# Even and odd projection columns in two tiles, values in long rows, the normalised input stored once: one change to a transformer layer on one core

## The reference

```
xn = (x - mean) / sqrt(var + 1e-5)
q, k, v = split(xn @ Wq + bq), split(xn @ Wk + bk), split(xn @ Wv + bv)
rope(x) = x * cos + rot(x) * sin          # rot: (even, odd) -> (-odd, even)
weights = softmax(rope(q) @ rope(k).T / sqrt(256))
attention = (weights @ v) @ Wo + bo
h = relu(s0 * [xn, -xn] @ w0) * 2;  h = relu(s1 * h @ w1) * 2;  ffn = s2 * h @ w2
out = x + attention + ffn
```

## Time and profile before

| | us |
|---|---|
| three runs | 2738.41, 2738.48, 2739.38 (median 2738.48) |
| the profiled run | 2738.91 |
| its span, first to last instruction | 2737.1 |

### The profile page before, as it was taken

One profiled execution on the slowest core, in us unless ns is written; L12 is line 12 of the kernel. 1 busy time (PEld: TensorE's weight loads), 2 busy tenths in 40 slices (PEclk: granted clock), 3 DMA queues, 4 the chain that ended last, 5 costly groups with the idle time before them and its releaser, 6 DMA issues.

```text
span 2737.1 us, 49717 instructions
## 1 busy us (share of the span) xinstructions
PE 2648.9 (97%) x21063; PEld 1397.6 (51%) x21063; DVE 989.5 (36%) x1655; ACT 2083.9 (76%) x2301; POOL 299.0 (11%) x265
## 2 busy tenths in 40 slices
PE   7999499999999999999999999999999999999997
PEld 5777245454444445454545454454545454544544
DVE  7776232324242323232342334242423323242322
ACT  4556388888888887878787878888787878787883
POOL 4666100000000000000000000000000000000000
PEclk9999699999999999999999999999999999999998
DMA  8888412212222222222221222221222222222213
GB/s 256 256 259 252 114 38 55 53 52 59 59 59 59 73 54 72 55 60 72 57 71 55 72 67 75 57 77 51 73 63 55 68 60 67 63 75 59 81 26 112
DMA packets 288416, 228.67 MB, mean 84 GB/s; under 512 B 184128, under 2 KB 227904, under 8 KB 281664
## 3 DMA queue, kind: packets, MB, share of 16 engines
q1 hardware_dynamic: 279744, 217.08, 29.0%
q10 hardware_dynamic: 8448, 8.39, 0.9%
HBM read 140.46 MB, written 84.93 MB: 82 GB/s over the span
## 4 chain that ended last, share of the span: by engine, by line
PE 86%; issue 1%; SPq 1%; DMA 1%; DVE 0%; POOLq 0%; POOL 0%; DVEq 0%
PE ps_o L930 35%; PE ps_f L963 26%; PE ps_s L915 23%; PE ps_y L978 2%; PE ps_f L1020 0%; SPq L810 0%; DMA xT_lo<-xn_lo_d 0%; DMA probs<-rest_sum_d 0%; PE ps_y L1020 0%; DVE k_rows L1115 0%; PE ps_o L1020 0%; SPq L807 0%; DVE sums L1060 0%; DMA heads_t<-heads 0%; SPq L709 0%
## 5 line engine op out<-in xcount | busy, mean ns | idle before, releaser
L895 ACT ACTIVATE probs<-ps_s 128x1024 f32<-128x1024 f32 x2048 | 1930.0, 1033 | 472.4 <-PE ps_s L915 470.1
L930 PE MATMUL ps_o<-probs,v_ones 128*32 128x512 f32 x8192 | 1011.9, 600 | 0.0
L915 PE MATMUL ps_s<-q_rows,k_rows 50*128 50x512 f32 x4096 | 866.3, 439 | 31.8 <-DMA q_rows<-row_shift 31.0
L915 PEld LDWEIGHTS ps_s<-q_rows,k_rows 50*128 50x128 f32 x4096 | 365.0, 184 | 701.9 <-ACT probs L895 600.0
L1077 DVE COPY raw<-ps_f 128x512 f32<-128x512 f32 x256 | 165.0, 686 | 790.8 <-PE ps_f L963 790.8
L930 PEld LDWEIGHTS ps_o<-probs,v_ones 128*32 128x32 f32 x8192 | 200.7, 109 | 418.5 <-issue 296.0
L963 PE MATMUL ps_f<-h_hi,ffn_w 64*128 64x512 f32 x2048 | 406.9, 393 | 0.0
L963 PE MATMUL ps_f<-h_lo,ffn_w 64*128 64x512 f32 x2048 | 405.8, 391 | 0.0
L1039 POOL TENSOR_TENSOR heads<-heads,sums 128x512 f32<-128x512 f32 x64 | 82.4, 1288 | 2147.9 <-DVE sums L1060 2147.9
L1060 DVE RECIPROCAL sums<-sums 128x128 f32<-128x128 f32 x256 | 226.7, 924 | 1.7
L963 PEld LDWEIGHTS ps_f<-h_lo,ffn_w 64*128 64x128 f32 x2048 | 195.8, 186 | 37.3
(11 more groups left out here) (102 smaller groups left out, 1616.5 us busy)
## 6 DMA issues: line engine op xcount, KB each, us to landing
k_rows<-k_parts SPq DMA_DIRECT2D x128, 256.0 KB
q_rows<-q_parts SPq DMA_DIRECT2D x384, 64.0 KB
q_parts<-parts SPq DMA_DIRECT2D x32, 512.0 KB, 3.7
k_parts<-parts SPq DMA_DIRECT2D x32, 512.0 KB, 5.5
k_rows<-k_parts SPq DMA_DIRECT2D x128, 128.0 KB
x_chunk<-in_x ACTq DMA_DIRECT2D x16, 512.0 KB, 6.0
xn_hi_d<-xn_hi SPq DMA_DIRECT2D x16, 512.0 KB, 4.4
xn_lo_d<-xn_lo SPq DMA_DIRECT2D x16, 512.0 KB, 5.2
```

The lines of the kernel that those rows point to most:

```text
L895: nc.scalar.activation(probs[:, s % PBUF, half * 2 * C:(half + 1) * 2 * C], ps_s[:, half].rearrange("p c n -> p (c n)"), ACT.Exp, scale=SC ...
L915: last = nc.tensor.matmul(ps_s[:, half, w], k_rows[rows, u, t * P:(t + 1) * P], q_rows[rows, u, half], start=True, stop=True)
L930: last = nc.tensor.matmul(ps_o[32 * c:32 * c + 2 * DH], v_ones[:, u, t], probs[:, s % PBUF, c * C:(c + 1) * C], start=(t == 0), stop=(t == ...
```

## The change

**Columns.** The weights are stored by even and odd columns: tile m = 0 holds the even, m = 1 the odd columns of all heads. One projection gives both tiles, in the two banks of ps_p, and each is the other's partner: `turned` is even x cos - odd x sin, then odd x cos + even x sin. The crossed copy of the weights and its projection go. A head is now 8 rows of the even and 8 rows of the odd tile, at two places of each scratch tensor, and `load_rows` reads them so. The order of a q tile's column blocks is permuted (COLUMNS) so that a half of the queries is one row of 4 KB.

**x.** ACT makes one more copy of the transposed x in float32 (`copy_x`), which is stored and loaded once. In attention DVE makes hi and lo of it (`split_x`) in round 24 of the pass before, and once ahead of the passes.

**v.** It has a PSUM bank of its own and is computed in two halves; its rows are stored 4 KB long, and each head's v is loaded by four DMAs.

**Statistics and FFN weights.** bn_aggr replaces five small DVE operations; statistics run one chunk further ahead; the FFN's weights are made in chunks 4 to 11, an eighth in each.

```diff
+FFN_WEIGHTS_AT = 4
+COLUMNS = [CB // 2 * (r % 2) + r // 2 for r in range(CB)]
+SPLIT_AT = 2 * len(BURSTS) + 4
...
             def store_x(c):
                 u = c % 2
-                sp.wait_ge(x_split, c + 1)
-                sp.dma_start(hi_out[c], x_hi[:, u].bitcast(F32)).then_inc(x_stored[u], 16)
-                sp.dma_start(lo_out[c], x_lo[:, u].bitcast(F32)).then_inc(x_stored[u], 16)
+                sp.wait_ge(x_copied, c + 1)
+                sp.dma_start(scratch["xn"][c], x_t[:, u].rearrange("p k n -> p (k n)")).then_inc(x_stored[u], 16)
...
+            def copy_x(c):
+                u = c % 2
+                if c >= 2:
+                    act.wait_ge(x_stored[u], 16 * (c // 2))
+                nc.scalar.activation(x_t[:, u].rearrange("p k n -> p (k n)"), ps_t[:].rearrange("p k n -> p (k n)"),
+                                     ACT.Copy).then_inc(x_copied, 1)
...
                 if n >= 2:
-                    pe.wait_ge(products_ready, n - 1)
-                for swapped in range(2):
+                    pe.wait_ge(products_ready, 2 * n - 2)
+                for m in range(2):
                     for k in range(DT):
-                        at = slice((j % DT) * P, (j % DT + 1) * P)
-                        w_hi, w_lo = wqk_hi[:, swapped, j // DT, k, at], wqk_lo[:, swapped, j // DT, k, at]
-                        to = ps_p[:, n % 2, swapped]
+                        w_hi, w_lo = wqk_hi[:, of, k, m], wqk_lo[:, of, k, m]
+                        to = ps_p[:, n % 2, m]
...
             for c in range(NC):
-                project(4 * c)
-                values(c)
+                project(2 * c)
+                if c + 1 < NC:
+                    turn(c + 1)
+                values(c, 0)
+                project(2 * c + 1)
+                values(c, 1)
                 if c > 0:
                     lengths(c - 1)
-                project(4 * c + 1)
-                project(4 * c + 2)
-                if c + 1 < NC:
-                    turn(c + 1)
-                project(4 * c + 3)
...
+                for t in range(TT):
+                    last = nc.vector.bn_aggr(moments[:, u, t], stats[:, u, t])
+                last.then_inc(var_ready, 1)
...
 def heads_of(scratch):
-    return (scratch[name].rearrange("a (g d) n -> g a d n", d=DH) for name in ("k", "q"))
+    return (scratch[name].rearrange("am (g e) n -> g am e n", e=HALF) for name in ("k", "q"))
...
         sp.dma_start(k_rows[at:at + 2 * DH, :].bitcast(F32), k_head[g]).then_inc(loaded, 16)
-        sp.dma_start(k_rows[at + 2 * DH:at + AUG, :].bitcast(F32), k_head[g, 0]).then_inc(loaded, 16)
-        sp.dma_start(q_rows[at:at + DH].bitcast(F32), q_half[g, 0, w]).then_inc(loaded, 16)
-        sp.dma_start(q_rows[at + DH:at + 2 * DH].bitcast(F32), q_half[g, 0, w]).then_inc(loaded, 16)
-        sp.dma_start(q_rows[at + 2 * DH:at + AUG].bitcast(F32), q_half[g, 1, w]).then_inc(loaded, 16)
-        sp.dma_start(q_rows[at + AUG:at + ROWS].bitcast(F32), shift[g, w]).then_inc(loaded, 16)
+        sp.dma_start(k_rows[at + 2 * DH:at + AUG, :].bitcast(F32), k_head[g, 0:2]).then_inc(loaded, 16)
+        sp.dma_start(q_flat[at:at + DH].bitcast(F32), q_head[g, 0:2, :, here]).then_inc(loaded, 16)
+        sp.dma_start(q_flat[at + DH:at + 2 * DH].bitcast(F32), q_head[g, 0:2, :, here]).then_inc(loaded, 16)
+        sp.dma_start(q_flat[at + 2 * DH:at + AUG].bitcast(F32), q_head[g, 2:4, :, here]).then_inc(loaded, 16)
+        sp.dma_start(q_flat[at + AUG:at + ROWS].bitcast(F32), shift[g, w]).then_inc(loaded, 16)
...
             def load_v(g, u):
-                sp.dma_start(v_ones[:, u, :, 0:DH], v_src[g]).then_inc(v_loaded[u], 16)
+                for r in range(CB):
+                    sp.dma_start(v_ones[:, u, r * TT:(r + 1) * TT, 0:DH], v_src[CB * (g // H) + r, :, g % H]).then_inc(v_loaded[u], 16)
 
             def load_x(i):
-                sp.dma_start(xT_hi[:].bitcast(F32), hi_src[i]).then_inc(xT_loaded, 16)
-                sp.dma_start(xT_lo[:].bitcast(F32), lo_src[i]).then_inc(xT_loaded, 16)
+                sp.dma_start(xT_lo[:].bitcast(F32).rearrange("p k n -> p (k n)"), scratch["xn"][i]).then_inc(xT_loaded, 16)
...
+            def split_x(i):
+
+                dve.wait_ge(xT_loaded, 16 * (i + 1))
+                nc.vector.tensor_copy(xT_hi[:], xT_lo[:].bitcast(F32)).then_inc(xT_high, 1)
+                dve.wait_ge(xT_high, i + 1)
+                nc.vector.tensor_tensor(xT_lo[:], xT_lo[:].bitcast(F32), xT_hi[:].bitcast(F32), ALU.subtract).then_inc(xT_split, 1)
...
+                    if n == SPLIT_AT and not last:
+                        split_x(i + 1)
```

More of the change, by code:

```diff
@@ L366, in _ @@
             high(0)
+            copy_x(0)
             deviation(1)
+            normalise(1)
+            deviation(2)
             act.wait_ge(weights_loaded, 16 * 6)
@@ L441, in lengths @@
                 for j in range(4):
-                    last = nc.tensor.matmul(ps_n[32 * j:32 * j + 32], per_head[:], square[:, c % 2, j], start=True, stop=True)
+                    rows = slice(32 * (j // 2), 32 * (j // 2 + 1))
+                    last = nc.tensor.matmul(ps_n[rows], per_head[:], square[:, c % 2, j], start=(j % 2 == 0), stop=(j % 2 == 1))
                 last.then_inc(norm_done, 1)
@@ L466, in _ @@
             pool.wait_ge(w_high, 1)
-            nc.gpsimd.tensor_tensor(wqk_lo[:, 0], wqk[:], wqk_hi[:, 0].bitcast(F32), ALU.subtract)
-            plain, crossed = (x.rearrange("p n k (m two) -> p n k m two", two=2) for x in (wqk[:], wqk_hi[:, 1]))
-            crossed_lo = wqk_lo[:, 1].rearrange("p n k (m two) -> p n k m two", two=2)
-            for side in range(2):
-                nc.gpsimd.tensor_tensor(crossed_lo[..., side], plain[..., 1 - side], crossed[..., side].bitcast(F32), ALU.subtract)
+            for m in range(2):
+                for n in range(2):
+                    nc.gpsimd.tensor_tensor(wqk_lo[:, n, :, m], of_pairs[:, n, :, :, m], wqk_hi[:, n, :, m].bitcast(F32), ALU.subtract)
             nc.gpsimd.tensor_tensor(wv_lo[:], wv[:], wv_hi[:].bitcast(F32), ALU.subtract).then_inc(w_split, 1)
@@ L483, in _ @@
                     pool.wait_ge(parts_ready, n - 2)
-                nc.gpsimd.tensor_tensor(turned[:, n % 3], by_cos[:, u], by_sin[:, u], ALU.add).then_inc(turn_done, 1)
+                nc.gpsimd.tensor_tensor(turned[:, n % 3], by_cos[:, u], by_sin[:, u], ALU.add if n % 2 else ALU.subtract).then_inc(turn_done, 1)
                 if n > 0:
@@ L574, in _ @@
             dve.wait_ge(weights_loaded, 16 * 6)
-            nc.vector.tensor_copy(wqk_hi[:, 0], wqk[:])
-            plain = wqk[:].rearrange("p n k (m two) -> p n k m two", two=2)
-            crossed = wqk_hi[:, 1].rearrange("p n k (m two) -> p n k m two", two=2)
-            for side in range(2):
-                nc.vector.tensor_copy(crossed[..., side], plain[..., 1 - side])
+            for m in range(2):
+                for n in range(2):
+                    nc.vector.tensor_copy(wqk_hi[:, n, :, m], of_pairs[:, n, :, :, m])
             nc.vector.tensor_copy(wv_hi[:], wv[:]).then_inc(w_high, 1)
-            nc.vector.stream_shuffle(bqk[:, 1], bqk[:, 0], [i ^ 1 for i in range(32)]).then_inc(bias_swapped, 1)
             low(0)
```

206 lines of the change are left out of this document (102 added, 104 removed).

## The result

| kernel | median us | runs | range |
|---|---|---|---|
| before | 2738.93 | 4 | 2738.41 to 2740.60 |
| changed | 2677.55 | 4 | 2675.63 to 2678.14 |

The ratio is 0.9774 (95% interval 0.9757 to 0.9791): the change makes the kernel 61.4 us faster. The forecast of 2739 was wrong, its range (2703 to 2768) too. The time is that of rival 1 (2674, given 0.08). All times here are medians of executions in the usual state; one execution of the kernel with its rows on eight engines took 7447.89 us, its five others 2665 to 2667, and it is left out.

What follows compares the result with a forecast made beforehand. TensorE was taken to bound attention and be nearly always busy in the preparation. From 2738.9 us, 66 less in the preparation, 6 more at attention's start and 60 more in 15 passes gave about 2739, no change; range 2703 to 2768.

Steps and rivals of the forecast that it cites:

- rival 1: Loads in attention stay on as many engines as before, x lands in time: 2674 us, faster; chance 0.08.
- Preparation, 66 us: Preparation before attention: chunks of 12.3 us instead of 16.3, the last three about 10.7; gain 66 us, ends 49 and 96.
- TensorE is no longer the bound: Preparation: with 60 instead of 84 instructions TensorE needs at most 10.9 us per chunk instead of 15.3.
- shift_ln, 0.16 or 1.31: DVE operation in the preparation's loop: 0.16 us, or 1.31 behind a GpSimd operation; chunk 11.6 to 12.8, 12.3 taken.
- Start, +6: Start of attention: head 0's rows come 6.4 us later, x is one load but needs 2.0 of split; ends 4 and 10.
- split_x, hidden: Attention passes: DVE's cast and subtract, 2.0 us per pass, are hidden if nothing else changes.
- The backlog, +6.35 (6.6 taken): Attention, head's loads of q and k: 152 KB more on each of two engines, x issued 6.35 us later, 6.6 taken.
- The stall, 3.4 - 0.2: Each attention pass: TensorE waits 3.4 us for the raw copies behind late x, ACT returns 0.2: 3.2 us.
- The clock, 0.8 a stall: Attention: TensorE's clock may fall after each stall, bounds 0 and 3.2 us per pass, a quarter taken: 0.8.

Runs made afterwards that it cites:

- the kernel with its rows on eight engines: Changed kernel with q and k rows of a head loaded from sources [8, 2, n], 14 loads per head instead of 12: 2666.04 us.
- the runs with more rows: Changed kernel with extra 14-row loads per half head into rows nothing reads: of k and q 2795.76 us, of k only 2750.82 us.
- the run with k alone: Changed kernel with one more load of k per half head, source [2, 7, 2048], into rows nothing reads: 2750.82 us.

## Why the prediction was wrong, point by point

- **Preparation, 66 us.** The size was right: 63.5. Counted with the order first, 17 of it come from the order, in which TensorE's repeated wait for xn_lo is gone, and 46 from the projections. The mean chunk is 12.3 to 12.5 us, as taken, but in part by luck. "TensorE is no longer the bound" was followed by a loop of ACT, DVE and GpSimd alone, in even chunks of 12.3 and three last ones of 10.7. Measured were, of the 15 spacings, nine of 11.4 to 12.5, five of 13.1 to 15.0 (in three of these DVE waited for the input) and a last one of 10.1. Transfers have a share in the loop (about 10 us for half a MB), and the forecast had only asked that they fit in 12.5.
- **shift_ln, 0.16 or 1.31.** 0.16 in 9 of 16 chunks and 0.27 to 1.25 in the others, 0.46 on average (0.65 in the stretch shown): nearer the short end than the middle that was taken. Neither it nor the falls of TensorE's clock in the preparation (0.98 and 0.99 in the stretches) was tested by itself. bn_aggr was hidden, as said, at 0.16 each.
- **Start, +6.** 2.2. The rows came 3.6 us later and not 6.4, by the same step as the backlog below, and the FFN's first matmul no longer waits for x.
- **split_x, hidden.** Right: 1.9 us on DVE in the pass, no wait of TensorE.
- **The backlog, +6.35 (6.6 taken): this step failed.** "On each of two engines 256/2 + 128/16 + 3x64/16 + 8/2 = 152 KB per half, 304 KB per head, 12.7 us" was wrong in its second to fourth terms: these loads, eight of ten spread over 16 engines, cost the two busy ones 4.9 us and not 1.9. The new total was right: 456 KB at 24.5 GB/s are 19.0 us, and the engines' work lasts from 1216 to about 1235. The sign was there to be read in the trace of before, where it lasts from 1279 to about 1296, 17 us, and my sum gave 12.7. I took the difference of two computed totals, when one of them could be measured.
- **The stall, 3.4 - 0.2.** It follows from the backlog. With 2.1 instead of 6.6 x is split at 1242.44, and both banks are free at 1243.6, before 1245.2. The mechanism itself is shown by the runs with more rows: a stall of 2.4 us with x 5.1 later than in the changed kernel, 4.8 with 7.1. The stall was mis-sized too: x 6.6 later than before is 4.5 later than in the changed kernel, and with 2.5 of that free about 2.0 would have been left, an estimate. x landed in 3.6 us and not 4.1, and TensorE's first matmul needs only the first of the two banks.
- **The clock, 0.8 a stall.** Mis-sized the other way: 2.3 to 2.7 beside each stall, of which the clock accounts for an estimated 1.8 to 2.5. With the predicted backlog a stall would then have cost about 2.0 + 2.3 = 4.3 us, near the 4.0 of the forecast, by two errors that nearly cancel. The kernel would have taken about 2677.5 + 15 x 4.3 + 3 for the start = 2745 us, an estimate from the run with k alone (2751 with 0.7 us more backlog), and "no change" would have come true. So the backlog alone decided it.
- **Rival 1** was given 0.08 since its reason, engines as many as before, spoke against the rows. The reason is refuted and the time came true: the case "fewer engines, but little backlog" had no rival of its own. The slack at x was about 2.5 us in the changed kernel and the predicted backlog 4.5 us more than the real one. So whether the kernel got 61 us faster or no faster hung on a transfer time that was computed and not read.
